# An attention and mixture-of-experts kernel on one core: who gates the unit tiles, and which columns of square roots GpSimd takes

## The reference, cut to what matters

```
# layer 0, attention: 16 heads of 8 channels, 4 batches -> 64 heads, each 1024 x 1024
d2   = max(q2[:, None] + k2[None, :] - 2 q k, 1e-12)
attn = softmax(-sqrt(d2));  out = attn @ v
# layer 0, feed-forward: a shared expert and one of 7 experts for each token
y_e  = (silu(h @ w1.T) * (h @ w3.T)) @ w2.T          # 128 -> 352 -> 128
# layer 1: ordinary softmax attention and a magnitude of two products
```

## Time and profile before

| | before |
|---|---|
| median of 3 runs | 1467.58 us (1466.52 to 1468.44) |
| the profiled execution's own time | 1466.36 us |
| its span | 1464.5 us |
| ACT busy | 1431.8 us, 98% |
| DVE busy | 1222.1 us, 83% |
| PE busy | 1112.9 us, 76% |
| POOL busy | 833.8 us, 57% |
| mean granted TensorE clock | 0.929 |

### The profile page before, as it was taken

The page is one execution under the profiler, slowest core; times in us unless marked ns, Lnnn a source line. Parts: engine busy times, 40 slices in busy tenths (PEclk is TensorE's granted clock), DMA queues, the critical chain, the costliest instruction groups (busy, mean ns, idle before and its releaser), DMA issues.

```text
span 1464.5 us, 22500 instructions
## 1 busy us (share of the span) xinstructions
PE 1112.9 (76%) x8231; PEld 464.9 (32%) x8260; DVE 1222.1 (83%) x2196; ACT 1431.8 (98%) x796; POOL 833.8 (57%) x737
## 2 busy tenths in 40 slices
PE   5588787788887877888879784777777677776766
PEld 3133234255153341543525411322223122221212
DVE  6998889977978979779797688858898898898886
ACT  3999999999999999999999999999999999999998
POOL 5188898878769788788788785622212033023100
PEclk8599899999998999989989997899999999999999
DMA  4942544222232325244262431043033033121020
GB/s 120 254 138 70 165 129 126 66 60 71 80 89 57 92 73 158 76 136 125 74 176 53 114 69 30 20 128 74 28 128 71 28 113 84 27 103 33 23 69 20
DMA packets 113185, 130.04 MB, mean 89 GB/s; under 512 B 42906, under 2 KB 81178, under 8 KB 113066
## 3 DMA queue, kind: packets, MB, share of 16 engines
q1 hardware_dynamic: 107738, 116.74, 29.5%
q0 software_dynamic: 4464, 11.09, 2.8%
q10 hardware_dynamic: 864, 0.69, 0.2%
HBM read 83.79 MB, written 44.70 MB: 88 GB/s over the span
## 4 chain that ended last, share of the span: by engine, by line
ACT 44%; issue 16%; PE 16%; DVE 15%; POOL 6%; DMA 1%; SPq 1%; another core or an unknown queue 0%; ACTq 0%; DVEq 0%; POOLq 0%
ACT scores L830 14%; ACT scores L791 11%; ACT exp L1352 11%; DVE scores L737 7%; PE pvb L718 6%; DVE exp L1360 5%; PE ring L703 4%; PE ring L1059 3%; ACT exp L1348 2%; PE ring L1070 2%; ACT scores L800 2%; POOL yro L1139 1%; DMA w<-in_w 1%; ACT L830 1%; ACT h L1091 1%
## 5 line engine op out<-in xcount | busy, mean ns | idle before, releaser
L737 DVE TENSOR_SCALAR scores<-ring 128x1024 f32<-128x1024 f32 x512 | 589.6, 1218 | 22.7 <-PE ring L703 18.8
L830 ACT ACTIVATE scores<-scores 128x8192 f32<-128x8192 f32 x63 | 438.9, 7022 | 0.2
L1352 ACT ACTIVATE exp<-ring 128x1024 f32<-128x1024 f32 x438 | 432.9, 1419 | 0.2
L1327 PE MATMUL ring<-stk 128*128 128x512 bf16 x995 | 299.6, 384 | 128.7 <-ACT exp L1352 103.6
L791 ACT ACTIVATE scores<-scores 128x7296 f32<-128x7296 f32 (+2 forms) x59 | 387.9, 6642 | 3.0 <-DVE scores L737 2.9
L718 PE MATMUL pvb<-scores,val 128*9 128x256 f32 x4096 | 326.2, 393 | 66.9 <-ACT scores L830 33.5
L1360 DVE SCALAR_TENSOR_TENSOR exp<-exp 128x512 f32<-128x512 f32 x438 | 322.7, 759 | 62.8 <-ACT exp L1352 56.6
L703 PE MATMUL ring<-stk 64*128 64x512 bf16 x1024 | 211.3, 410 | 69.1 <-DVE scores L737 56.9
L1327 PEld LDWEIGHTS ring<-stk 128*128 128x128 bf16 x1024 | 65.7, 97 | 338.5 <-ACT exp L1352 233.4
L703 PEld LDWEIGHTS ring<-stk 64*128 64x128 bf16 x1024 | 49.9, 93 | 306.7 <-DVE scores L737 206.1
L718 PEld LDWEIGHTS pvb<-scores,val 128*9 128x9 f32 x4096 | 65.2, 89 | 190.1 <-issue 185.6
(11 more groups left out here) (263 smaller groups left out, 1474.8 us busy)
## 6 DMA issues: line engine op xcount, KB each, us to landing
stk<-stack SPq DMA_DIRECT2D x192, 192.0 KB, 2.9
w<-in_w SPq DMA_DIRECT2D x39, 352.0 KB, 3.5
w<-in_w SPq DMA_DIRECT2D x39, 192.0 KB, 2.9
stack<-qp SPq DMA_DIRECT2D x7, 768.0 KB, 4.3
stack<-kp SPq DMA_DIRECT2D x7, 768.0 KB, 5.4
xj<-xg SPq DMA_DIRECT2D x10, 448.0 KB
yg<-xj POOLq DMA_DIRECT2D x10, 448.0 KB
stack<-qp SPq DMA_DIRECT2D x7, 512.0 KB, 5.1
```

Of the source, the lines that this page charges most:

```text
L737: nc.vector.tensor_scalar(S[place][:, j * N:(j + 1) * N], tile, 1e-12, None, ALU.max).then_inc(o.release(("qk", group, place, j)), 1)
L830: nc.scalar.activation(S[place][:], S[place][:], ACT.Exp, scale=-1.0).then_inc(exp_done, 1)
L1327: mm = nc.tensor.matmul(out[:, cols], stk1[place][:, Q, i * P:(i + 1) * P], stk1[place][:, K, cols], start=True, stop=True)
L1352: nc.scalar.activation(EX[k // 2][:, k % 2, :], tile, ACT.Exp, scale=SCALE1).then_inc(o.release(("qk1", n, i)), 1)
```

## The change

- GpSimd's two gating instructions go. VectorE gates with one instruction, gate = (h1 + 1) * gate over 128 x 2688 elements, right after step 8 (`GATE_AT`) of rounds 4 to 13.
- GpSimd takes the root of 448 columns of place 0 in rounds 4 to 13. Pieces of 448 and 448 in a place become one of 896. In some rounds a place gets 448 columns more.
- The token tiles are turned after step 28 (`TOKENS_AT`), by TensorE and by VectorE's copy, in rounds 4 to 12. The second product comes straight after step 31, ahead of place 3's turned output, on both engines.
- The second product's weights are loaded at places 0 and 1, the first product's at places 1, 2 and 3, and the tokens ahead of both at place 1.
- The clearing of `stk1` moves from round 14 to after the last piece of round 15.

```diff
-    ((), (896,), (448, 448), (448,)),     # round 3
-    ((), (896,), (), ()),
-    ((), (448, 448), (), ()),
-    ((), (896,), (448, 448), ()),
-    ((), (896,), (448, 448), (448,)),     # rounds 7 to 13
...
-    ((), (448, 448), (448, 448), ()),
-    ((), (448, 448), (448,), ()),
+    ((), (896,), (896,), (448,)),         # round 3
+    ((448,), (896,), (), ()),
+    ((448,), (448, 448), (), ()),
+    ((448,), (896,), (896,), (448,)),
+    ((448,), (896,), (896,), (896,)),     # rounds 7 to 13
...
+    ((), (896,), (896,), (448,)),
+    ((), (896,), (896,), (448,)),
...
-        def pool_hidden(pool, v):
-            n = v - FIRST_JOBS + 1
-            pool.wait_ge(tanh_done, n)
-            nc.gpsimd.tensor_scalar(h1[:, :, :], h1[:, :, :], 1.0, 1.0, ALU.add, ALU.mult).then_inc(part_done, 1)
-            pool.wait_ge(part_done, n)
-            nc.gpsimd.tensor_tensor(gate[:, :, :], gate[:, :, :], h1[:, :, :], ALU.mult).then_inc(hid_done, 1)
+        def dve_gate(dve, v):
+            dve.wait_ge(tanh_done, v - FIRST_JOBS + 1)
+            nc.vector.scalar_tensor_tensor(out=gate[:, :, :], in0=h1[:, :, :], scalar=1.0, in1=gate[:, :, :],
+                                           op0=ALU.add, op1=ALU.mult).then_inc(hid_done, 1)
...
+        TOKENS_AT, GATE_AT = CHG - 4, CH
+        DOWN_AT = [range(0, 4), range(4, JOBS), (), ()]
+        UP_AT = [(), range(0, 1), range(1, 5), range(5, JOBS)]
...                                          # TensorE, round r
+                        if FIRST_JOBS < r <= LAST_JOBS and s == TOKENS_AT:
+                            pe_tokens(pe, o, r)
+                    if FIRST_JOBS < r <= LAST_JOBS + 1:
+                        pe_down(pe, o, r - 1)
                     if r:
                         pe_turn_out0(pe, r - 1, GROUP - 1)
...
-                    if FIRST_JOBS <= r <= LAST_JOBS:
+                    if r == FIRST_JOBS:
                         pe_tokens(pe, o, r)
-                    if FIRST_JOBS < r <= LAST_JOBS + 1:
-                        pe_down(pe, o, r - 1)
                     if FIRST_JOBS <= r <= LAST_JOBS:
                         pe_up(pe, o, r)
...                                          # SyncE
-                            jobs = range(2 * place, min(2 * place + 2, JOBS))
...
+                        if ROUTED_JOBS + 1 < r <= LAST_JOBS + 1:
+                            load_down_weights(sp, o, r - 1, DOWN_AT[place])
+                        if ROUTED_JOBS < r <= LAST_JOBS:
+                            load_up_weights(sp, o, r, UP_AT[place])
...                                          # GpSimd, round r
-                    if FIRST_JOBS < r <= LAST_JOBS + 1:
-                        pool_hidden(pool, r - 1)
                     if r == PLACE_ROUND:
                         pool_place(pool, o, chain)
+                    pool_roots(pool, o, roots, r, 0)
                     if r == ADD1_ROUND:
                         pool.wait_ge(y_stored, Y_ALL)
                         pool_gather(pool, 0)
-                        clear_stacks1(pool)
...
                     pool_roots(pool, o, roots, r, 3)
+                    if r == TURN1_ROUND:
+                        roots.wait()
+                        clear_stacks1(pool)
...                                          # VectorE, round r
+                        if FIRST_JOBS < r <= LAST_JOBS + 1 and s == GATE_AT:
+                            dve_gate(dve, r - 1)
+                        if FIRST_JOBS < r <= LAST_JOBS and s == TOKENS_AT:
+                            dve_keep_tokens(dve, o, r)
+                    if FIRST_JOBS < r <= LAST_JOBS + 1:
+                        dve_keep_down(dve, o, r - 1)
                     if r:
                         dve_divide(dve, r - 1, GROUP - 1)
```

More of the change, by code:

```diff
@@ L126 @@
     ((), (896,), (448,), ()),
-    ((), (896,), (448, 448), (448,)),
-    ((), (896,), (), ()),
-    ((), (448, 448), (), ()),
-    ((), (896,), (448, 448), ()),
-    ((), (896,), (448, 448), (448,)),
-    ((), (896,), (448, 448), (448,)),
-    ((), (896,), (448, 448), (448,)),
-    ((), (896,), (448, 448), (448,)),
-    ((), (896,), (448, 448), (448,)),
-    ((), (896,), (448, 448), (448,)),
-    ((), (896,), (448, 448), (448,)),
-    ((), (448, 448), (448, 448), ()),
-    ((), (448, 448), (448,), ()),
+    ((), (896,), (896,), (448,)),
[3 more added lines that the diff above has]
+    ((448,), (896,), (896,), (896,)),
+    ((448,), (896,), (896,), (896,)),
+    ((448,), (896,), (896,), (896,)),
+    ((448,), (896,), (896,), (896,)),
+    ((448,), (896,), (896,), (896,)),
+    ((448,), (896,), (896,), (896,)),
+    ((448,), (896,), (896,), (896,)),
+    ((), (896,), (896,), (448,)),
+    ((), (896,), (896,), (448,)),
 ]
@@ L362, in build @@
             sem("r_" + n) for n in ("router_in", "clipped", "odds_ready", "chosen", "routed", "tok_in", "placed"))
-        w_in, up_in, down_in, xj_in, h1_done, gate_done, tanh_done, part_done, hid_done, y_out, y_stored = (
-            sem("j_" + n) for n in ("w_in", "up_in", "down_in", "xj_in", "h1_done", "gate_done", "tanh_done", "part_done",
+        w_in, up_in, down_in, xj_in, h1_done, gate_done, tanh_done, hid_done, y_out, y_stored = (
+            sem("j_" + n) for n in ("w_in", "up_in", "down_in", "xj_in", "h1_done", "gate_done", "tanh_done",
                                     "hid_done", "y_out", "y_stored"))
@@ L769, in pool_roots @@
                 o.emptied(pool, ("qk", group, place, (first + width - 1) // N))
-                y, h, x = scratch[:, 0:width], scratch[:, width:2 * width], S[place][:, first:first + width]
+                y, h, x = scratch[:, 0:width], scratch[:, ROOT_WIDTH:ROOT_WIDTH + width], S[place][:, first:first + width]
                 chain.step(nc.gpsimd.tensor_scalar(y.bitcast(I32), x.bitcast(I32), -0.5, SEED_BITS, ALU.mult, ALU.add))
@@ L1931, in fast @@
                                 load_own_tokens(sp)
-                        if ROUTED_JOBS < r <= LAST_JOBS + 1:
-                            jobs = range(2 * place, min(2 * place + 2, JOBS))
-                            if r <= LAST_JOBS:
-                                load_up_weights(sp, o, r, jobs)
-                            if r > ROUTED_JOBS + 1:
-                                load_down_weights(sp, o, r - 1, jobs)
                         if place == 1:
@@ L1940, in fast @@
                                 load_jobs(sp, o, r, r - 1 - FIRST_JOBS)
+                        if ROUTED_JOBS + 1 < r <= LAST_JOBS + 1:
+                            load_down_weights(sp, o, r - 1, DOWN_AT[place])
+                        if ROUTED_JOBS < r <= LAST_JOBS:
+                            load_up_weights(sp, o, r, UP_AT[place])
+                        if place == 1:
                             if r == LAST_JOBS + 1:
@@ L2065, in general @@
                 for v in range(FIRST_JOBS, LAST_JOBS + 1):
-                    pool_hidden(pool, v)
                     pool_store_jobs(pool, o, v)
@@ L2262, in general @@
                     dve_keep_up(dve, o, v)
+                    dve_gate(dve, v)
                     dve_keep_down(dve, o, v)
@@ L2297, in fast @@
                             dve_clip(dve, o)
-                    if FIRST_JOBS <= r <= LAST_JOBS:
+                    if r == FIRST_JOBS:
                         dve_keep_tokens(dve, o, r)
-                    if FIRST_JOBS < r <= LAST_JOBS + 1:
-                        dve_keep_down(dve, o, r - 1)
                     if FIRST_JOBS <= r <= LAST_JOBS:
```

## The result

The changed kernel took 1470.18 us as the median of 20 executions (1466.95 to 1476.31); the kernel before took 1467.95 in its 20 beside them (1466.40 to 1470.05). The ratio is 1.0025, with a 95% interval of 1.0018 to 1.0031. It became slower, by 2.2 us of the medians, where I had forecast a gain of 1 us. The profiled execution took 1468.95 us with a span of 1467.3, against 1466.36 and 1464.5.

What follows compares the result with a forecast made beforehand. ScalarE bounded the rounds at 58.7 us; the change made VectorE's loop 58.3. Round gains of 2.7, nearly lost at layer 1's start, with half the odd hole gave -1.0: profiled 1465.4, plus 1.2 is 1466.6 us, range 1460.5 to 1473.

Steps and rivals of the forecast that it cites:

- the loop from exponential to exponential: Place 0's exponential, VectorE's maxima, place 3's root, next exponential: 54.5 us before, forecast 58.3 in rounds 7 to 12.
- the stretch: VectorE's time from a round's first maximum to its last: 38.4 us before, forecast 42.5 with the gate.
- X(12): X(r) is when place 0's exponential of round r ends; for round 12 the forecast was 779.4 us.
- the third rival: Round's end stays long: slow second product or late first-product weights make VectorE's and TensorE's loop 59.5; 1476 us, chance 0.07.
- The second rival: GpSimd holds up VectorE's gate after step 8, rounds 4 to 12: gate 4.1 us, kernel 1475.6, chance 0.17.
- one odd hole: Round 14: VectorE's unexplained 3.08 us standstill, about 1.8 for ScalarE; its return taken as half likely, sum -1.0.
- the sum of rounds 14 and 15: Rounds 14 and 15 gain 0.4 + 0.8 us by columns, bringing the sum to -2.7 before the start of layer 1.
- the start of layer 1: Later clearing delays the split 6.2 us, so ScalarE waits 2.6 for the first tile and the gain is 0.1.
- covered, by 0.3 us only: VectorE's and TensorE's loop between first maxima, 58.0 us, stays hidden under the 58.3 us exponential-to-exponential loop.
- ScalarE stays the bound: First rival: gate and token copy fall into VectorE's spare time; about -7 us, 1460.6, chance 0.18.
- The holes go: Fourth rival: VectorE's holes in rounds 5, 6, 9 and 14 vanish; 1462 us, chance 0.08.

Runs made afterwards that it cites:

- k12: The changed kernel once more, unaltered, as one execution for a second profile: 1473.19 us.
- k4: The changed kernel with round 14's eight gathers moved behind place 1's piece: 1471.3 us, ratio 1.0048.
- k5: k3 with round 14's gathers split, four behind place 0's piece and four behind place 1's: 1467.9 us, ratio 1.0004.
- k6: The kernel before with only round 14's gathers split four and four: 1463.4 us, ratio 0.9977.
- k10: k9 with round 14's gathers split four and four: 1462.4 us, ratio 0.9970.
- k13: k10 with the change's new order of TensorE and SyncE added, gate still on GpSimd: 1462.8 us, ratio 0.9972.
- k14: The changed kernel with only round 14's gathers split four and four: 1468.1 us, ratio 1.0010.
- k7: The changed kernel with the gate on 64 columns of one unit tile, the rest left out: 1464.0 us, ratio 0.9978.
- k9: The kernel before with only GpSimd's 448 columns of place 0 added in rounds 7 to 13, gate still on GpSimd: 1466.6 us, ratio 0.9998.
- k2: The changed kernel with rounds 14 and 15 as before (pieces and clearing): 1470.2 us, ratio 1.0026.
- k3: The changed kernel with stk1 cleared before round 15's stores and no place 3 piece in round 15: 1467.9 us, ratio 1.0015.
- k1: The changed kernel with GpSimd's pieces and the clearing as before, keeping VectorE's gate and the new order: 1482.2 us, ratio 1.0106.
- k8: The kernel before with only TensorE's and SyncE's new order, gate still on GpSimd: 1467.1 us, ratio 1.0002.
- k11: The changed kernel with the gate on three of its seven unit tiles, the rest left out: 1464.2 us, ratio 0.9983.

## Why the prediction was wrong, step by step

**Right: the loop from exponential to exponential.** The gate was put at 3.1 and took 2.95; the stretch at 42.5, it took 42.3; the round at 58.3, it took 58.07, with ScalarE waiting 0.1 where I had said 0.4. X(12) was put at 779.4 and came at 779.0; X(13) at 837.3, it came at 837.0. That these agree so well is luck in part: X(6) came 1.1 later than the sum had it, and rounds 7 to 12 took 1.4 less. The second product ran at once, in 5.0 us and not 6.4 (so the third rival is out), and the wait of round 4 (1.8) came as forecast. The second rival's price didn't come in that profile: where gate and GpSimd met, GpSimd was the one held up (3.17 for 0.57), which costs nothing. The rule of the Trainium skill that I drew on (SBUF — State Buffer, "Who interferes with whom": the later of the two blocks) agrees with these rows: the gate had begun 0.19 us before. It agrees with k12's round 8 too, where GpSimd's instruction had begun at 505.01, 0.19 us before the gate, and the gate took 3.76.

**Wrong: "one odd hole", and with it the sum of rounds 14 and 15.** I took it for chance whether the hole of 3.08 us returns, and booked half of its price as a gain. It is tied to the gathers, which stayed as they were: it moves with them (k4), and goes, or shrinks to 0.97 (k5), when they are issued four at a time (k6, k10, k13, k14). It not only came back: VectorE stood still for 2.31 + 2.81 instead of 0.60 + 3.08. That lengthened the stretch from 42.4 to 44.5 us, and ScalarE, with 0.4 us less work of its own, waited 4.75 instead of 2.1. Forecast: X(14) 2.9 us earlier (1.6 by X(13), 0.4 by columns, 0.9 by the hole). Measured: 0.4 later, although X(13) was 2.0 earlier. These 3.3 us are nearly the whole miss of the profile, 3.6 (1468.95 against 1465.4).

Why the two holes are longer than before isn't shown. The gathers began 3.9 us after the round's first maximum, where it had been 5.1. But other profiles with eight in a row have 3.7 (before) to 5.3 us (k7) without following that start: k9, whose gathers began at 5.8, has 1.74 + 3.06, and k2 at 3.9 has 1.73 + 2.74. The kernel before's trace, from which I took the price, is the mildest of them.

**Nearly right in kind, under-sized: the start of layer 1.** I put ScalarE's wait at 2.6 and had it hidden by rounds that ended 3.6 us earlier. Layer 1 lost 3.1 between the last exponential and tile 24, and there was nothing to hide it in. The clearing took 4.61 us, where I had 3.7. In k3, whose profile has the same rounds, this step (with round 15's piece of place 3) is worth 2.7 us: it ends at +0.14 instead of +2.8. The medians say 2.2 (1470.2 and 1467.9), but the intervals of the two ratios overlap.

**Missing: that a loop without slack has a spread.** I priced the loop with one number and added "covered, by 0.3 us only". The executions of the changed kernel spread over 9 us; with the gate halved, over 4. The other kernels with the full gate and the wider pieces (k2 to k5, k14) spread over 6.4 to 9.8, all kernels with a shorter gate or with the gate on GpSimd over 5.0 or less, the kernel before over 5.5 at most; only k1, with four executions, has 0.7. k12, one of the longer ones, was 6.8 us behind the first profile at X(10) and 4.2 at the end. Before, this loop was 54.5 against ScalarE's 58.7, and the slack took such things up: in k6, whose middle rounds are the kernel before's, first maxima come 4.3 and 4.8 us after the exponential in rounds 12 and 13, and ScalarE waits for nothing. By medians the gate's length costs about 6 us with the wider pieces (k7) and its move 15 without (k1 against k8, the rows of scatters with it), the order nothing (k8), the clearing about 2 (k3), and the eight gathers in a row 2 (k14) to 4 (k10 against k9). The wider pieces had to carry all of that.

**The rivals.** "ScalarE stays the bound" was not the case with the whole gate; with half or none of it (k11, k7) it was, at 57.94 us a round. "The holes go" came out the other way in round 14. In rounds 5, 6 and 9 no hole of 0.3 us is left, but the stretches of rounds 5 and 6 took 1.4 and 0.4 us more than those of the full rounds, at the lower clock.

## What to carry to other kernels

A move of 3 us onto an engine that has idle time on average can take all slack from the one loop that closes over it. Compare the loops round by round, and ask of each not only whether it is longer than the bound but by how much it is shorter, because a hole in a loop without slack is passed on from round to round. And before giving a stall whose releaser has no name even odds, look at what the other engines issue in that time, and match each tile's product with its copy: that says which of two engines really waits.

## What the runs showed of the hardware

- While GpSimd issued eight indirect gathers in a row in round 14, VectorE started its latest copy 4.9 us (k4) to 7.0 us (the changed kernel, k3, k7, k9) after the end of the product, by the profile, with holes of 2.3 + 2.8 us in the changed kernel, 0.6 + 3.1 before, 1.2 + 3.1 in k4 and 4.0 in one in k8. TensorE's pause of 2.13, marked "issue", ended 0.05 us after VectorE had freed a ring tile. Rows of eight or more scatters gave holes of 1.6 + 2.4 and 2.0 (k1).
- Rows of four gathers in round 14 (k5, k6, k10, k13, k14) left one hole of 0.97 (k5) and otherwise none over 0.4. Where a row of four lies over the start of round 5 or 6, the kernels before, k6, k9 and k10 have holes of 0.6 to 1.1 there.
- Eight in a row don't always do it: in layer 1 the same row (996.7 to 1007.7 before, 999.1 to 1010.5 in the changed kernel) left TensorE no idle time over 0.4 us. The mechanism wasn't tested.
- VectorE's gate, with two SBUF inputs, and GpSimd's root instructions held each other up, the later one each time: 3.17 for 0.57 on GpSimd's side, 3.76 for 2.95 and 2.22 for 1.35 (k11) on VectorE's. VectorE's eight additions of line 1188, also with two SBUF inputs, took 2.18 us alone (before, k3) and 5.96 to 6.63 under a piece of GpSimd (k14, k5, k4).
- The same stretch of TensorE, after the same 2.84 us of waiting, ran at a granted clock of 1.00 in one execution and partly at the lower level in another; eight small products took 0.62 or 1.04 us.
